# Twelve of the sixteen tiles of a fused macaron layer: unrolled code against a register loop of two tiles

## What is computed

```python
x = x + 0.5 * ffn(layernorm(x))          # 128 -> 512 -> 512 -> 128
x = x + attn(layernorm(x))               # 16 heads of 8, with its own residual and layernorm
x = x + 0.5 * ffn(layernorm(x))          # the same ffn again

def ffn(x):                              # weights are +1 or -1 from boolean masks
    h = relu(s0 * (concat([x, -x]) @ W0)) * 2
    h = relu(s1 * (h @ W1)) * 2
    return s2 * (h @ W2)

def attn(x):
    ctx = softmax(Q @ K.T / sqrt(8)) @ V          # per sequence and head
    return layernorm(ctx + x) * gamma + beta
```

## Time and profile before

| | |
|---|---|
| median of 3 runs | 940.36 us (934.2 to 945.82) |
| the profiled execution | 945.82 us, of which 944.0 us lie between its first and last instruction (the span) |
| mean granted clock of TensorE | 0.911 of full speed |
| PE busy | 840.9 us, 89% of the span |
| DVE, ACT, POOL busy | 76%, 60%, 36% of the span |

### The profile page before, as it was taken

One profiled execution on the slowest core, in us unless ns is written; L12 is line 12 of the kernel. 1 busy time (PEld: TensorE's weight loads), 2 busy tenths in 40 slices (PEclk: granted clock), 3 DMA queues, 4 the chain that ended last, 5 costly groups with the idle time before them and its releaser, 6 DMA issues. The chain is left out here.

```text
span 944.0 us, 19082 instructions
## 1 busy us (share of the span) xinstructions
PE 840.9 (89%) x7258; PEld 354.7 (38%) x7258; DVE 722.0 (76%) x1610; ACT 562.2 (60%) x995; POOL 339.6 (36%) x471
## 2 busy tenths in 40 slices
PE   6568979999999999999899999999999999878976
PEld 2232324444343434444333444434343444233332
DVE  5636777988888887988877787888787788767643
ACT  3123756666666757666656666666676666556742
POOL 4521052533434242534424253442433253432331
PEclk8875969999998989999977999999897999797997
DMA  2000101010100001010100101010100100010000
GB/s 58 12 33 18 31 10 38 13 36 13 42 18 32 27 23 37 14 46 4 40 17 25 34 17 43 13 35 13 37 22 27 34 18 31 1 38 11 13 1 23
DMA packets 28746, 23.58 MB, mean 25 GB/s; under 512 B 5616, under 2 KB 28656, under 8 KB 28656
## 3 DMA queue, kind: packets, MB, share of 16 engines
q1 hardware_dynamic: 28656, 22.37, 7.4%
HBM read 5.05 MB, written 4.19 MB: 10 GB/s over the span
## 5 line engine op out<-in xcount | busy, mean ns | idle before, releaser
L785 ACT ACTIVATE probs<-ps_t,score_scale 128x512 f32<-128x512 f32 x512 | 344.3, 685 | 159.7 <-PE ps_t L630 159.4
L1001 DVE TENSOR_REDUCE row_max<-ps_s 128x2 f32<-128x512 f32 x512 | 344.4, 684 | 78.8 <-PE ps_s L616 76.2
L753 ACT ACTIVATE ffn_hi<-ps_z 128x512 f16<-128x512 f32 x288 | 171.7, 597 | 137.8 <-PE ps_z L543 75.8
L952 DVE SCALAR_TENSOR_TENSOR ffn_lo<-ps_z,ffn_hi 128x512 f16<-128x512 f32 x256 | 176.4, 689 | 97.7 <-ACT ffn_hi L753 93.2
L542 PE MATMUL ps_z<-ffn_hi,w 128*128 128x512 f16 x512 | 201.1, 393 | 11.8 <-DVE ffn_lo L952 11.8
L616 PE MATMUL ps_s<-k_rows,q_rows 24*128 24x256 f16 x1024 | 196.7, 290 | 16.5 <-DMA k_rows<-k_hi 10.3
L630 PE MATMUL ps_t<-q_rows,k_rows 26*128 26x256 f16 x1024 | 192.6, 287 | 15.0 <-DMA q_rows<-max_rows 11.5
L543 PE MATMUL ps_z<-ffn_lo,w 128*128 128x512 f16 x512 | 198.6, 388 | 0.0
L650 PE MATMUL ps_c<-probs,v_cols 128*32 128x256 f32 x2048 | 147.8, 409 | 0.2 <-ACT max_rows L791 0.2
L616 PEld LDWEIGHTS ps_s<-k_rows,q_rows 24*128 24x128 f16 x1024 | 52.9, 94 | 169.5 <-issue 77.0
L438 POOL TENSOR_TENSOR att_ve<-att_mv,eps 128x4 f32<-128x4 f32 x16 | 3.2, 201 | 245.3 <-DVE att_mv L935 245.3
(11 more groups left out here) (113 smaller groups left out, 1036.3 us busy)
## 6 DMA issues: line engine op xcount, KB each, us to landing
x<-L_attn_x SPq DMA_DIRECT2D x16, 256.0 KB, 2.7
q_rows<-q_hi SPq DMA_DIRECT2D x128, 32.0 KB
k_rows<-k_hi SPq DMA_DIRECT2D x128, 32.0 KB
q_rows<-max_rows SPq DMA_DIRECT2D x256, 2.0 KB
y<-x SPq DMA_DIRECT2D x16, 256.0 KB, 2.1
q_rows<-q_lo SPq DMA_DIRECT2D x64, 32.0 KB
k_rows<-k_lo SPq DMA_DIRECT2D x64, 32.0 KB
k_raw<-L_ffn_k SPq DMA_DIRECT2D x1, 256.0 KB, 3.1
```

The source lines that it names most:

```text
L753: a_.activation(ffn_hi[:, use, :], ps_z[use % 2][:], ACT.Relu if use else ACT.Copy, scale=1.0 if use else XN_SCALE).then_inc(z_hi, 1)
L785: a_.activation(probs[grp % 2][:, softmax_lane(u), :], ps_t[u % 2][:], ACT.Exp, scale=score_scale[:, 0:1]).then_inc(s_exp, 1)
L952: v.scalar_tensor_tensor(out=ffn_lo[:, use, :], in0=ps_z[use % 2][:], scalar=0.0, in1=ffn_hi[:, use, :], op0=ALU.max, op1=ALU.subtract).th ...
L1001: v.tensor_reduce(row_max[u // HB % 2][:, j::LANES, g % 2], ps_s[u % 2][:].rearrange("p (a k) -> p a k", a=2), AX.X, ALU.max).then_inc(s_m ...
```

## The change

`run` no longer unrolls t = 2 to 13. It opens a counted loop of six trips on each engine, whose body is two iterations, one per buffer parity. The tile number becomes an expression of the loop's register: `pair * 2 + 2` and `pair * 2 + 3`. So does all that is worked out from it: the values of the waits, the numbers of the ffns and of the misc uses, and on SP the addresses of load and store. Head and tail are as before, and so are the compute instructions, their shapes, their order on each engine and all buffers. (The new file also has 13 empty lines at its top, so its line numbers up to the loop are higher by 13, and after it by 14.)

```diff
             for it in head:
                 steps(it)
-            for t in range(LOOP_FROM, LOOP_TO):
-                steps(full(t, t % 2))
+            with eng.Fori(0, (LOOP_TO - LOOP_FROM) // 2) as pair:
+                for r in range(2):
+                    steps(full(pair * 2 + (LOOP_FROM + r), r))
             for it in tail:
                 steps(it)
```

## The result

| | before | after |
|---|---|---|
| median | 940.62 us (934.2 to 945.82, 4 runs) | 981.57 us (979.42 to 984.24, 4 runs) |
| ratio, 95% interval | | 1.0455 (1.0399 to 1.0512) |
| span of the profiled execution | 944.0 us | 983.6 us |

The looped code is 4.5% slower. The forecast was 966 us, the measured time lies in its range, and about six tenths of the loss were forecast. Medians here are of all executions, ratios leave disturbed ones out. All 20 executions of the looped kernel on record lie between 976.1 and 997.6 us.

What follows compares the result with a forecast made beforehand. PE was taken as the bound, with SP's queue pacing each tile's second half. Branches 5, waits 7, SP 2.4 and clock 11 sum to 25.4 us on 940.4, giving 966 us, own range 950 to 990, 8-in-10 range 938 to 1,010.

Steps and rivals of the forecast that it cites:

- The sign and the place: Slower by over 2% (0.59); gap before first `scores` or `shifted` 1 us longer at every second tile's end, five times.
- The branch term: PE at the loop's end: code refetch of 2.6 us, about 1.6 covered, 1.0 exposed per branch, 5 us in all.
- The clock term: Longer PE gaps lower the clock; all 12 tiles become like the 54.2 us tile (mean clock 0.91): 11 us, -13 to +60.
- The waits: Register instructions at 158 waits per tile on PE, mostly hidden: 0.6 us per tile, 7 us in all, 0 to 95.
- SP's 2.4 us: Waits and registers in the busy half of SP's queue, which ends the tile: 0.2 us per tile, 0 to 12 x 1.
- DVE's stall at nothing: At the loop's end DVE waits for PE and takes its own stall beside it, costed at nothing.
- The rival "everything is covered": Loop-end stall and register instructions stay hidden, only SP's 2.4 us shows: 943 us, 936 to 950; chance 32%.
- The rival with broken run-ahead: Register waits hold PE's sequencer until met, each of 158 exposing its handling: 1,025 us, 990 to 1,100; chance 9%.
- Faster: Later `scores` and `shifted` close the mid-tile gap, all tiles run at clock 1.00 in 52.2 us: 921 us; chance 4%.

Runs made afterwards that it cites:

- pe_head_at_block_start: The looped kernel with the first instruction of PE's loop moved to the start of a 16 KB fetch block: 968.6 us, 1.0268 of the kernel before.
- registers_unrolled: The kernel before, still unrolled, but PE, DVE, ACT and POOL take the tile number from a register loaded once: 944.9 us, 1.0044 of before.
- hint_and_block_start: The looped kernel with a branch-back hint each trip and every engine's loop head at a fetch block's start: 941.9 us, 1.0003 of the kernel before.

## Why the prediction was right, and where it fell short

*The sign and the place* were right: the loss sits at every second tile's end, five times and not twelve, in gaps ahead of the first `scores` and `shifted`, with more packets on the fetch queues, and it is slower by over 2%.

*The branch term* is the step that was mis-sized: "5 x 1.0 = 5 us, between 0 and 5 x 3.1 = 15.5". Measured, 20 us of new gaps, outside its bounds. Three things were wrong. I took 2.6 us for the fetch at the branch and 3.1 at most; the branch's record lasts 3.4 to 4.0. I counted one fetch, and it was two, since the target lay just ahead of a block's end; pe_head_at_block_start shows it. And I let 1.6 us be covered. What is queued ahead of the array covered 1.2 at each branch, which left the gap of 2.9. The idle time that was there is another matter: the maxima's gap went when the branch's came, since the maxima landed meanwhile, which saves 1.5 us per branch out of 5.5.

*The clock term*, 11 us by way of the 54.2 us tile, was the right mechanism with the size too small: PE is busy 16 us longer for the same work. I had spread it over 12 tiles by tenths of a microsecond. It came at five places, where PE worked for 2.4 to 2.9 of 8 us.

*The waits*, 7 us, are 1 to 7 by registers_unrolled (4 at its middle) and within 4 of nothing by hint_and_block_start. I counted one register instruction per wait, 158 per tile on PE; the program has 88. None of PE's gaps in registers_unrolled is one of issue. With fewer of them PE's body has 2,012 instructions and not some 2,100, so it does not just miss fitting but just fits, and it was fetched again all the same: in pe_head_at_block_start nine blocks moved per trip for a body of eight.

So where the sum has 5 + 7 + 2.4 + 11, the runs show some 20, 4 at most, nothing for SP, and 16. The errors partly offset one another: the branch term is 15 us short and the clock term 5, and the waits and SP are over 5 us too high.

*SP's 2.4 us* was not measured by itself. SP's four small DMAs at the tile's end and the load behind them are 0.75 us apart now (265.03 to 265.78) and not 0.05, where nobody waits; with SP and three others unrolled the time was no lower, so SP gave nothing that shows.

*DVE's stall at nothing* holds beside PE's, as argued, and not without it.

*The rival "everything is covered"* needed a refetch under 1.6 us. By the Trainium skill's "Advanced Engine Details and Errata", Engine Queue Depths, a queue of 64 would give cover; here the array went on for 1.2 us behind the branch, against an estimated 1.9 us, and the gaps of 2.9 us are what was left. *The rival with broken run-ahead* falls with registers_unrolled: waits on registers did not stall PE. *Faster* had nothing for it.

## What to carry to other kernels

A loop on an engine's sequencer is paid at its branch back, not at its waits: here 8 us for each, about half in late code and half in the low clock behind it, against some 4 us at most for all register instructions together. Before looping, count the body's instructions against the engine's blocks, and see where its head and its branch stand in theirs; a hint at the top and the head on a block boundary brought the same loop to 1.0003 of the unrolled code. When a new stall falls where an old gap was, take the longer of the two, and then ask what the clock does after it.

## What the runs showed that was not expected

Code that has run once can be kept: with the hint and eight blocks, PE ran its trips of 2,013 instructions without one fetch after the first (22 packets in all), and without the hint each trip fetched nine blocks, from the same aligned place (67). The place of a loop within a block decided between one gap and two (968.6 and 981.6 us), and so 29 against 115 instructions between a block's start and the branch decided between a gap of 2.2 us and none. The lines of code ahead of a loop shift that place, so an edit there can move the time of a loop that it doesn't touch; that is concluded, not tried.

A stall of 2 us on DVE, an engine with 24% of its time free, cost some 9 us over five branches where PE had no stall of its own. With PE's own stalls gone and DVE's left, the same kernel took 942 us in one execution and 965 in another; what makes the difference is open.
